# Expert-choice stage with up and down products of two experts alternated on TensorE

## The chip, the cores and the metric

One core of a Trainium2 chip runs the whole kernel. Times are device microseconds of one execution; the kernel before was run three times.

## The reference, cut

The kernel computes two gated transformer layers over 8 x 256 tokens of 256 features: attention, capacity experts, dilated attention, and last the expert-choice stage, the only one that the change touches:

```python
Sm = softmax(xf @ Wr + br)              # 2048 tokens, 8 experts
G_t, idx_t = top_k(Sm.T, 256)           # each expert takes its 256 best tokens
tokens = xf[idx]
Wu = W_up[arange(8) // 2]               # two experts of a group share the up weights
mid = silu(einsum('keh,ehf->kef', tokens, Wu) + bu)      # 256 -> 682
out = einsum('kef,efh->keh', mid, W_down) + b_down       # 682 -> 256
y = zeros_like(xf).at[idx].add(G[..., None] * out)
```

## The kernel before

`experts_choice` (L1895) is the fourth stage. Its first part finds each expert's threshold over the 2048 probabilities by a search in eight levels on VectorE (L2170 to L2192), then ranks the tokens. The weights are loaded on SP meanwhile; SP's first load waits until GpSimd has zeroed `bu_in` and `w2` (L2056, L2057), and VectorE's search starts after constants of GpSimd and after the bias table `buT`, which needs SP's three first loads.

The second part handles eight experts. Products are made exact enough by splitting each float32 operand into a float16 high and low part and multiplying three times (high by high, high by low, low by high). The weights are scaled by 256 before the split.

`pipeline` (L2008) is shared by all engines. It issues `step(e, u, g, slots, rows, products)`: two steps ahead of the loop, a device loop of three iterations with two steps each, two steps behind it. In step e each engine does its share of

- `slots` of expert e + 2: VectorE marks token positions (`at_lo` L2255, `at_hi`, `vhi`), TensorE multiplies them (16 small products into `ps_i`, L2369), VectorE turns the result into indices (`g_idx` L2293, a copy `who` L2294), GpSimd gathers the token rows (L2088);
- `rows` of expert e + 1: ScalarE splits up and down weights (L2132) and VectorE takes their low parts (L2273); TensorE turns the gathered rows in two tiles of 128 tokens (L2362) into the two banks `ps_y`, ScalarE and VectorE split them (L2136, L2278); VectorE copies gate and bias columns (L2283, L2287);
- `products` of expert e: six chunks f of the 682 hidden features. TensorE makes 6 up products of 256 columns per chunk (L2351) into four banks `ps_h`, ScalarE applies silu and copies the high part (L2121, L2126), VectorE takes the low part (L2268). Then TensorE makes 2 x 18 down products (L2384), VectorE adds the bias (L2303), ScalarE scales by the gate (L2142), GpSimd adds the rows into the output with two indirect transfers (L2098).

Every engine runs its instructions in the order of the code. On TensorE that is up(e), with the turning of e + 1 between chunks, slots of e + 2, down(e). The down products wait for the hidden low parts of the same expert, and the second token tile of `ps_y` for the split rows, since `ps_x` and `ps_y` are the same banks. ScalarE and VectorE do weight splits between the chunks f (after f = 0 and 2; f = 1 and 3). There is one `hh`, one `hl`, one `yb`, one `y`, one staging `w1` and one `w2`; SP loads the next pair of weights when both low parts are done.

Of the kernel before, what the change touches and what calls it, by code (L numbers as in the profile page):

```python
# [15 lines left out]
F16 = mybir.dt.float16  # L16
BF16 = mybir.dt.bfloat16
I32 = mybir.dt.int32
# [1876 lines left out]
def experts_choice(nc, S, ins, dram, keep, out):  # L1895
# [7 lines left out]
    LEVELS = [26, 22, 18, 14, 10, 6, 2, 0]  # L1903
    WS = 256.0
    FIRST = 4
    assert GRP == 16 and LAST and E // G == 2 and TAKE <= 512
    ident, ones, tg, prob = keep["ident"], keep["ones"], keep["tg"], keep["prob"]
    with ExitStack() as ctx:
# [52 lines left out]
        g_idx = [sb(f"g_idx{u}", [P, CT], I32) for u in range(2)]  # L1961
        s_idx = [sb(f"s_idx{u}", [P, CT], I32) for u in range(2)]
        who = sb("who", [P, E, CT])
        xg = [sb(f"xg{u}", [P, CT, S.ROW]) for u in range(2)]
        gate = [sb(f"gate{u}", [P, CT]) for u in range(2)]
        b1 = [sb(f"b1{u}", [P, FC]) for u in range(2)]
# [3 lines left out]
        w2 = sb("w2", [P, FC, D])  # L1970
# [4 lines left out]
        h = [sb(f"h{k}", [P, TAKE]) for k in range(2)]  # L1975
        hh = sb("hh", [P, FC, TAKE], F16)
        hl = sb("hl", [P, FC, TAKE], F16)
        yb = sb("yb", [P, CT, D])
        y = sb("y", [P, CT, D])
# [6 lines left out]
        ps_x = [ps_y[k][:, 0:C * P].rearrange("p (c t) -> p c t", c=C) for k in range(2)]  # L1986

        s_cst = sem("cst"); s_byA = sem("byA"); s_abv = sem("abv"); s_si = sem("si"); s_ldb = sem("ldb")
# [8 lines left out]
        s_g = [sem("g0"), sem("g1")]; s_w = sem("w"); s_gate = sem("gate"); s_b1 = sem("b1")  # L1997
        s_px = sem("px"); s_xh = sem("xh"); s_xl = sem("xl"); s_wh = sem("wh"); s_wl = sem("wl")
# [3 lines left out]
        def pipeline(step):  # L2002


            def run(eng):
                step(-2, 0, 0, True, False, False)
                step(-1, 1, 0, True, True, False)
                with eng.Fori(0, E // 2 - 1) as i:  # L2008
                    step(i * 2, 0, i, True, True, True)
                    step(i * 2 + 1, 1, i + 1, True, True, True)  # L2010
                step(E - 2, 0, G - 1, False, True, True)
                step(E - 1, 1, G, False, False, True)
            return run

        def count(eng, what, value):

            if not isinstance(value, int) or value > 0:
                eng.wait_ge(what, value)

# [11 lines left out]
        def _(sp):  # L2031
            bu = ins["L1_ffn_b_up"]
            sp.wait_ge(s_fill, 2)
# [4 lines left out]
            def load(e, g):  # L2038
                sp.dma_start(w1[:], ins["L1_ffn_W_up"][g].rearrange("(c p) f -> p c f", p=P)).then_inc(s_w, 16)
                down = ins["L1_ffn_W_down"][e]  # L2040
                sp.dma_start(w2[:, 0:FULL, :], down[0:FULL * P, :].rearrange("(c p) d -> p c d", p=P))\
                    .then_inc(s_w, 16)
                sp.dma_start(w2[0:LAST, FULL, :], down[FULL * P:F, :]).then_inc(s_w, 16)

            load(0, 0)

            def step(e, u, g, slots, rows, products):
                if rows and not (isinstance(e, int) and e + 2 >= E):
                    sp.wait_ge(s_wl, (e + 2) * 2)
                    load(e + 2, g + 1 if u == 0 else g)  # L2050

            pipeline(step)(sp)

        @block.gpsimd
        def _(pool):
            pool.memset(bu_in[:], 0.0).then_inc(s_fill, 1)  # L2056
            pool.memset(w2[:], 0.0).then_inc(s_fill, 1)  # L2057
# [23 lines left out]
            def step(e, u, g, slots, rows, products):  # L2081
                if slots:
                    pool.wait_ge(s_gi, (e + 3) * 2)
                    count(pool, s_px, (e + 1) * CT)
                    count(pool, s_gate, e + 1)
                    apart(pool, s_pass)
                    for j in range(CT):
                        pool.indirect_dma_start(  # L2088
                            out=xg[u][:, j, :], out_offset=None, in_=dram["rows"],
                            in_offset=bass.IndirectOffsetOnAxis(ap=g_idx[u][:, j:j + 1], axis=0))\  # L2090
                            .then_inc(s_g[u], 16)
                if products:
                    count(pool, s_add, e * CT * 16)
                    pool.wait_ge(s_si, e + 1)
                    for j in range(CT):
                        pool.wait_ge(s_y, e * CT + j + 1)
                        apart(pool, s_pass)
                        pool.indirect_dma_start(  # L2098
                            out=flat_out, out_offset=bass.IndirectOffsetOnAxis(ap=s_idx[u][:, j:j + 1], axis=0),
                            in_=y[:, j, :], in_offset=None, compute_op=ALU.add).then_inc(s_add, 16)  # L2100

            pipeline(step)(pool)
# [3 lines left out]
        def _(act):  # L2106
            act.wait_ge(s_pt, 2)
            for k in (1, 3):
                act.wait_ge(s_pt, k + 1)
                act.activation(byexp[:, k * 512:(k + 1) * 512], ps_t[:, k, :], ACT.Copy).then_inc(s_byA, 1)  # L2110

            def step(e, u, g, slots, rows, products):
                v = 1 - u
                if products:
                    act.wait_ge(s_b1, e + 1)
                for f in range(FC):
# [321 lines left out]
```

## Time and profile before

| | |
|---|---|
| median of 3 runs | 938.09 us (936.34 to 939.6) |
| the profiled execution, own time | 939.1 us |
| its span, first to last instruction | 937.4 us |
| mean granted TensorE clock | 0.833 |
| busy: TensorE, VectorE, ScalarE, GpSimd | 654.0, 528.3, 427.8, 338.0 us |
| first up product of the expert-choice stage | 798.1 us |

The page divides the span into 40 slices; the product part of the last stage is the last six (23.4 us each). A digit is the busy share in tenths:

```profile
PE   3999983145999999999324877788877301757755
DVE  0467753625656666564025578877755387555651
ACT  1344430034567775576112546566555110564652
PEclk9999995557999999999755788998888555787877
```

### The profile page before, as it was taken

What the parts mean: (1) busy time and instruction counts of PE and PEld (TensorE: products, weight loads), DVE (VectorE), ACT (ScalarE), POOL (GpSimd) and SP (SyncE); (2) the same over time, 40 slices, a digit from 0 to 9 for tenths busy, and PEclk for the clock granted to TensorE, in tenths of its full rate; (3) what the DMA queues carried; (4) which work ended last, traced back from release to release, by engine and by line L of the source; (5) the groups of instructions that cost most, each with busy time, mean ns of one, the idle gap of its engine ahead of it and who ended that gap; (6) DMA issues with size and microseconds to landing.
All of it is one profiled execution on the core that took longest, in us unless ns stands there. A gap on an engine that the chain in (4) does not pass through costs nothing. (4 is left out here: it accounts for less than half of the span.)

```text
span 937.4 us, 15352 instructions
## 1 busy us (share of the span) xinstructions
PE 654.0 (70%) x4856; PEld 486.4 (52%) x4856; DVE 528.3 (56%) x1701; ACT 427.8 (46%) x847; POOL 338.0 (36%) x473
## 2 busy tenths in 40 slices
PE   3999983145999999999324877788877301757755
PEld 3888872123877778777212444455445200545543
DVE  0467753625656666564025578877755387555651
ACT  1344430034567775576112546566555110564652
POOL 1244431053653466452212444544433201323422
PEclk9999995557999999999755788998888555787877
DMA  5132321334453455441311212332100110435332
GB/s 174 45 124 84 121 91 45 125 94 134 103 136 82 121 130 113 126 78 23 50 40 41 70 42 80 92 93 62 45 25 34 71 59 14 146 89 153 89 86 23
DMA packets 74955, 78.66 MB, mean 84 GB/s; under 512 B 8101, under 2 KB 66513, under 8 KB 74641
## 3 DMA queue, kind: packets, MB, share of 16 engines
q1 hardware_dynamic: 62305, 62.11, 21.0%
q0 software_dynamic: 10928, 15.57, 9.7%
q8 instruction: 28, 0.46, 0.2%
q10 hardware_dynamic: 1664, 0.27, 0.2%
q14 instruction: 30, 0.25, 0.1%
HBM read 54.99 MB, written 22.94 MB: 83 GB/s over the span
## 5 line engine op out<-in xcount | busy, mean ns | idle before, releaser
L1650 DVE CUSTOM_DVE_ANT_0 c_sn<-c_ps_s,k_mask 128x128 f32<-128x128 f32 (+1 forms) x256 | 75.8, 352 | 57.7 <-PE c_ps_s L1788 57.6
L1174 PE MATMUL b_ps_y<-b_w2h,b_hh 128*128 128x256 f16 x320 | 87.3, 273 | 4.5 <-DVE b_xl L1050 4.2
L924 POOL DMA_INDIRECT res<-b_y,b_s_idx x40 | 72.7, 1816 | 42.4 <-ACT b_y L966 30.8
L1174 PE MATMUL b_ps_y<-b_w2l,b_hh 128*128 128x256 f16 x320 | 87.2, 273 | 0.0
L1174 PE MATMUL b_ps_y<-b_w2h,b_hl 128*128 128x256 f16 x320 | 87.2, 273 | 0.0
L910 POOL DMA_INDIRECT b_xg<-rows,b_g_idx x40 | 43.8, 1094 | 119.7 <-DVE b_g_idx L1068 110.0
L1482 POOL TENSOR_SCALAR_AFFINE_SELECT c_pr<-c_pr 128x512 f32<-128x512 f32 x64 | 42.9, 671 | 111.0 <-ACT c_pr L1541 110.0
L1041 DVE TENSOR_TENSOR b_hl<-b_h,b_hh 128x640 f16<-128x640 f32 x64 | 52.8, 825 | 36.9 <-ACT b_hh L946 36.7
L1816 PE MATMUL c_ps_v<-c_pr,k_vx 128*64 128x256 f32 (+1 forms) x512 | 64.0, 377 | 5.5 <-POOL c_pr L1482 4.9
L1139 PE MATMUL b_ps_h<-b_xh,b_w1h 128*128 128x320 f16 x256 | 57.1, 305 | 12.7 <-ACT b_h L941 9.3
L941 ACT ACTIVATE b_h<-b_ps_h,b_b 128x640 f32<-128x640 f32 x64 | 50.1, 784 | 18.8 <-DVE b_hl L1041 11.6
L1541 ACT ACTIVATE c_pr<-c_ps_t 128x768 f32<-128x768 f32 x64 | 51.7, 807 | 13.2 <-PE c_ps_t L1802 13.2
L1139 PE MATMUL b_ps_h<-b_xl,b_w1h 128*128 128x320 f16 x256 | 56.9, 304 | 0.0
L1139 PE MATMUL b_ps_h<-b_xh,b_w1l 128*128 128x320 f16 x256 | 56.9, 304 | 0.0
L2384 PE MATMUL d_ps_y<-d_w2h,d_hh 128*128 128x256 f16 x96 | 34.2, 357 | 31.2 <-DVE d_xl L2278 30.9
L1788 PE MATMUL c_ps_s<-k_ks,c_qs 48*128 48x128 f16 (+1 forms) x256 | 25.3, 282 | 43.4 <-DVE c_mx L1650 27.9
L2088 POOL DMA_INDIRECT d_xg<-rows,d_g_idx x16 | 18.6, 1165 | 98.1 <-DVE d_who L2294 95.6
L966 ACT ACTIVATE b_y<-b_yb,b_gate 128x256 f32<-128x256 f32 x40 | 20.3, 508 | 72.6 <-DVE b_yb L1087 72.6
L1816 PEld LDWEIGHTS c_ps_v<-c_pr,k_vx 128*64 128x64 f32 x512 | 34.6, 152 | 30.7 <-issue 12.6
L946 ACT ACTIVATE b_hh<-b_h 128x640 f16<-128x640 f32 x64 | 47.2, 737 | 2.3
L2098 POOL DMA_INDIRECT out_dram<-d_y,d_s_idx x16 | 29.5, 1845 | 37.3 <-ACT d_y L2142 30.2
L1788 PEld LDWEIGHTS c_ps_s<-k_ks,c_qs 48*128 48x128 f16 x256 | 10.1, 104 | 51.5 <-DVE c_mx L1650 21.0
(382 smaller groups left out, 1812.2 us busy)
## 6 DMA issues: line engine op xcount, KB each, us to landing
b_w<-in_L_ffn_W_dram SPq DMA_DIRECT2D x16, 1024.0 KB, 5.6
d_w<-in_L_ffn_W_up_dram SPq DMA_DIRECT2D x8, 682.0 KB
d_w<-in_L_ffn_W_down_dram SPq DMA_DIRECT2D x8, 640.0 KB
k_ks<-kT SPq DMA_DIRECT2D x48, 64.0 KB, 2.5
c_qs<-q SPq DMA_DIRECT2D x48, 64.0 KB, 2.3
rows<-a_rows SPq DMA_DIRECT2D x8, 264.0 KB, 2.5
rows<-c_rows SPq DMA_DIRECT2D x8, 264.0 KB, 2.2
a_x_in<-in_x_dram SPq DMA_DIRECT2D x8, 256.0 KB, 3.0
```

What stands on the lines that cost most here:

```text
L910: pool.indirect_dma_start(out=xg[u][:, j, :], out_offset=None, in_=dram["rows"], in_offset=bass.IndirectOffsetOnAxis(ap=g_idx[u][:, j:j + ...
L924: pool.indirect_dma_start(out=dram["res"], out_offset=bass.IndirectOffsetOnAxis(ap=s_idx[u][:, j:j + 1], axis=0), in_=y[:, j, :], in_offse ...
L941: act.activation(h[f % 2][:], ps_h[f % 2][:, :, 0:HALF], ACT.Gelu, bias=b1[u][:, f:f + 1], scale=1.0 / WS).then_inc(s_h, 1)
L946: act.activation(hh[:, f, :], h[f % 2][:].rearrange("p a b -> p (a b)"), ACT.Copy)\
L1041: dve.tensor_tensor(hl[:, f, :], h[f % 2][:].rearrange("p a b -> p (a b)"), hh[:, f, :], ALU.subtract).then_inc(s_hl, 1)
L1139: last = pe.matmul(ps_h[f % 2][:, t, 0:HALF], a, b[:, c, t * HALF:(t + 1) * HALF], start=(c == 0 and k == 0), stop=(c == C - 1 and k == 2))
L1174: last = pe.matmul(ps_y[(j + CT) % 2][:, 0:D], a, b[:, f, :], start=(f == 0 and k == 0), stop=(f == FC - 1 and k == 2))
L1482: pool.affine_select(out=late, in_=late, compare_op=ALU.is_ge, fill=0.0, base=0, pattern=[[0, 2], [0, 2], [1, P]], channel_multiplier=-1). ...
L1541: act.activation(pr[i % 2][:], ps_t[:, :, 0:QK], ACT.Exp).then_inc(s_pr, 1)
L1650: dve.tensor_tensor_reduce(sn[r][:, a:b], ps_s[:, r, a:b], mask[:, a:b], -1.0, 3.0e38, ALU.add, ALU.min, mx[g % 2][:, q, r, j:j + 1]).then ...
L1788: last = pe.matmul(ps_s[:, r, lo:hi], q[a:a + 3 * HD, j, rows_], key[a:a + 3 * HD, j, 0:keys], start=True, stop=True)
L1816: last = pe.matmul(ps_v[VW * r:VW * (r + 1), 0:b - a], vx[n % 2][:, part, 2 * j + r, :], pr[i % 2][:, r, a:b], start=(part == 0), stop=(pa ...
```

## The change

The assertions now ask for 2 token tiles, an even number of chunks, and 512 columns for `C * TAKE`. `pipeline` and the device loop go: every engine's order is written for e from -1 to 7 with Python loops, and all instructions are unrolled. TensorE's order is up(e+1), turn(e+2), slots(e+3), down(e). Chunks are handled in pairs: two silus, one copy and one subtraction of 2 x 256 columns. The rows of an expert are turned in one go into the bank `ps_r` and split whole. The up split is made once per group of two experts. The gate is read from the gathered rows and the bias from `buT` by ScalarE itself; the scatter uses the same index tile as the gather. There are now two each of `w2`, `hh`, `hl`, `y`, four of `xg`, five of `g_idx`, and one `w1` as before. ScalarE runs one silu on a single column at the start of the stage. The diff, cut:

```diff
@@ tiles and banks
+        g_idx = [sb(f"g_idx{u}", [P, CT], I32) for u in range(5)]
+        xg = [sb(f"xg{u}", [P, CT, S.ROW]) for u in range(4)]
         w1 = sb("w1", [P, C, F])
-        w2 = sb("w2", [P, FC, D])
+        w2 = [sb(f"w2{u}", [P, FC, D]) for u in range(2)]
-        h = [sb(f"h{k}", [P, TAKE]) for k in range(2)]
+        h = [sb(f"h{k}", [P, 2, TAKE]) for k in range(2)]
+        hh = [sb(f"hh{u}", [P, FC, TAKE], F16) for u in range(2)]
+        hl = [sb(f"hl{u}", [P, FC, TAKE], F16) for u in range(2)]
+        yb = [sb(f"yb{j}", [P, D]) for j in range(CT)]
+        y = [sb(f"y{u}", [P, CT, D]) for u in range(2)]
-        ps_x = [ps_y[k][:, 0:C * P].rearrange("p (c t) -> p c t", c=C) for k in range(2)]
+        ps_x = ps_r[:, 0:C * TAKE].rearrange("p (c t) -> p c t", c=C)
@@ SP
-            sp.wait_ge(s_fill, 2)
+            sp.wait_ge(s_fill, 3)
...
+            load_up(0)
+            load_down(0)
+            load_down(1)
+            for e in range(E):
+                if e % 2 == 0 and group(e) + 1 < G:
+                    sp.wait_ge(s_wl1, group(e) + 1)
+                    load_up(group(e) + 1)
+                if e + 2 < E:
+                    sp.wait_ge(s_wl2, e + 1)
+                    load_down(e + 2)
@@ GpSimd
-            pool.memset(w2[:], 0.0).then_inc(s_fill, 1)
+            for u in range(2):
+                pool.memset(w2[u][:], 0.0).then_inc(s_fill, 1)
...
+            def gather(e):
+                pool.wait_ge(s_gi, e + 1)
+                count(pool, s_y, (e - 3) * CT)
...
+            def scatter(e):
+                count(pool, s_add, e * CT * 16)
+                for j in range(CT):
+                    pool.wait_ge(s_y, e * CT + j + 1)
...
+            for e in range(-3, E):
+                if e + 3 < E:
+                    gather(e + 3)
+                if e >= 0:
+                    scatter(e)
@@ ScalarE
+            act.wait_ge(s_warm, 1)
+            act.activation(warm[:], warm[:], ACT.Silu)
+
+            def up_high(g):
+                act.wait_ge(s_w1, (g + 1) * 16)
+                count(act, s_ph, (g - 1) * 2 * FC)
+                act.activation(w1h[g % 2][:], w1[:], ACT.Copy, scale=WS).then_inc(s_wh1, 1)
+
+            def down_high(e):
+                act.wait_ge(s_w2[e % 2], (e // 2 + 1) * 32)
+                count(act, s_py, (e - 1) * CT)
+                act.activation(w2h[e % 2][:], w2[e % 2][:], ACT.Copy, scale=WS).then_inc(s_wh2, 1)
+
+            def hidden(e, p):
...
+                for q in range(2):
...
+                    act.wait_ge(s_ph, e * FC + f + 1)
+                    if q == 0:
+                        count(act, s_hl, n - 1)
+                    act.activation(h[n % 2][0:r, q, :], ps_h[f % 4][0:r, 0:TAKE], ACT.Silu,
+                                   bias=buT[0:r, f * G + group(e):f * G + group(e) + 1], scale=1.0 / WS)\
+                        .then_inc(s_h, 1)
+                act.wait_ge(s_h, e * FC + 2 * p + 2)
+                count(act, s_py, (e - 1) * CT)
+                act.activation(hh[e % 2][:, 2 * p:2 * p + 2, :], h[n % 2][:], ACT.Copy).then_inc(s_hh, 1)
...
+            up_high(0)
+            act.wait_ge(s_buT, 1)
+            rows_high(0)
+            for e in range(-1, E):
+                if e + 1 < E:
+                    for p in range(PAIRS):
+                        hidden(e + 1, p)
+                    if e + 2 < E:
+                        rows_high(e + 2)
+                    down_high(e + 1)
+                    if e % 2 == 1 and group(e + 3) < G:
+                        up_high(group(e + 3))
+                if e >= 0:
+                    scaled(e)
@@ VectorE
+            def found(e):
+                dve.wait_ge(s_pidx, e + 1)
+                count(dve, s_add, (e - 4) * CT * 16)
+                dve.tensor_scalar(g_idx[e % 5][:], ps_i[:, 0:CT], -1.0, 0.0, ALU.add, ALU.max).then_inc(s_gi, 1)
...
+            marked(0)
+            found(0)
+            marked(1)
+            up_low(0)
+            found(1)
+            marked(2)
+            rows_low(0)
+            for e in range(-1, E):
+                if e + 4 < E:
+                    marked(e + 4)
+                if e + 1 < E:
+                    hidden_low(e + 1, 0)
+                if e >= 0:
+                    down_low(e)
+                if e + 1 < E:
+                    hidden_low(e + 1, 1)
+                if e >= 0 and e % 2 == 0 and group(e + 2) < G:
+                    up_low(group(e + 2))
+                if e + 1 < E:
+                    hidden_low(e + 1, 2)
+                if e + 2 < E:
+                    rows_low(e + 2)
+                if e + 3 < E:
+                    found(e + 3)
+                if e >= 0:
+                    biased(e)
@@ TensorE
+            def hidden(e):
+                g = group(e)
+                pe.wait_ge(s_xl, e + 1)
+                pe.wait_ge(s_wl1, g + 1)
+                for f in range(FC):
+                    r = rows_of(f)
+                    count(pe, s_h, e * FC + f - 3)
...
+            def down(e):
+                pe.wait_ge(s_wl2, e + 1)
+                for j in range(CT):
+                    count(pe, s_yb, (e - 1) * CT + j + 1)
+                    for f in range(FC):
+                        r = rows_of(f)
+                        if j == 0 and f % 2 == 0:
+                            pe.wait_ge(s_hl, e * PAIRS + f // 2 + 1)
...
+            found(0)
+            found(1)
+            turned(0)
+            for e in range(-1, E):
+                if e + 1 < E:
+                    hidden(e + 1)
+                if e + 2 < E:
+                    turned(e + 2)
+                if e + 3 < E:
+                    found(e + 3)
+                if e >= 0:
+                    down(e)
```

Helpers not shown: `rows_high` and `rows_low` split `ps_x` with one instruction each; `marked` issues `at_lo`, `at_hi` and `vhi`; `up_low` and `down_low` are the weights' low parts; `hidden_low(e, p)` is the low part of a pair of chunks; `biased` and `scaled` handle the two token tiles of a result, `biased` waiting for the end of each tile's down products; `turned` makes four transposes after its gather has landed.

## Rows read from the trace of the kernel before

**Rows 1.** Two loop steps: length; busy PE, PEld, DVE, ACT, POOL; clock; DMA share; GB/s.

```profile
817.20:851.90 34.70, 24.23 (x186) 17.12 (x184) 19.52 (x41) 19.02 (x38) 11.65 (x8) 0.80 0.44 112
```

**Rows 2.** Chain of waits, last stage: start us, length, what.

```profile
789.51 0.88 issue
...
820.96 1.47 ACT d_w2h L2132
...
823.61 0.80 DVE d_w2l L2273
...
826.09 7.25 PE d_ps_y L2384 x36
```

**Rows 3.** Windows of 1 us; columns as in rows 1, the clock third from last.

```profile
806.00:807.00 1.00, 0.49 (x17) 0.40 (x15) 0.55 (x2) 0.97 (x3) 0.00 (x0) 1.00 0.00 0
808.00:809.00 1.00, 0.00 (x0) 0.00 (x0) 1.00 (x3) 0.57 (x2) 0.00 (x0) 0.60 0.00 0
831.00:832.00 1.00, 1.00 (x6) 0.74 (x5) 0.14 (x1) 0.51 (x1) 0.00 (x0) 0.50 0.52 137
832.00:833.00 1.00, 1.00 (x10) 0.68 (x8) 0.00 (x0) 0.00 (x0) 0.39 (x1) 0.95 0.04 13
```

**Rows 4.** Timeline of TensorE: start us, length, idle before.

```profile
798.14 0.39 PE L2351 MATMUL d_ps_t<-d_xh,d_w1h 128*128 128x256 f16 x1 [0.53 <-DVE d_xl L2278]
...
801.32 0.31 PE L2351 MATMUL d_ps_t<-d_xh,d_w1h 128*128 128x256 f16 x1
...
802.88 0.27 PE L2351 MATMUL d_ps_t<-d_xh,d_w1l 128*128 128x256 f16 x1
804.54 0.44 PE L2362 MATMUL d_ps_y<-ident,d_xg 128*128 128x128 f32 x2 [1.39 <-DMA d_xg<-rows,d_g_idx]
...
805.95 0.54 PE L2369 MATMUL d_ps_i<-d_vhi,d_at_lo 128*128 128x2 f16 x16
```

**Rows 5.** Groups by line and shape: count, busy, mean ns, idle before.

```profile
L2121 ACT ACTIVATE d_h<-d_ps_t,d_b 128x256 f32<-128x256 f32 x40 | 18.3, 457 | 0.0
L2255 DVE TENSOR_TENSOR d_at_lo<-d_lane,d_lo 128x2048 f16<-128x2048 f16 x8 | 18.3, 2286 | 0.5 <-issue 0.4
L2268 DVE TENSOR_TENSOR d_hl<-d_h,d_hh 128x256 f16<-128x256 f32 x40 | 16.9, 423 | 17.8 <-ACT d_hh L2126 17.8
L2126 ACT ACTIVATE d_hh<-d_h 128x256 f16<-128x256 f32 x40 | 16.7, 416 | 1.5
L2273 DVE SCALAR_TENSOR_TENSOR d_w2l<-d_w,d_w2h 128x1536 f16<-128x1536 f32 x8 | 14.0, 1752 | 0.0
...
L2283 DVE COPY d_gate<-d_xg 128x2 f32 x6 | 0.9, 151 | 0.0
...
L1041 DVE TENSOR_TENSOR b_hl<-b_h,b_hh 128x640 f16<-128x640 f32 x64 | 52.8, 825 | 36.9 <-ACT b_hh L946 36.7
```

**Rows 6.** ScalarE's table loads (window from 735 us); SP's issue of one pair of weights.

```profile
L2121 ACT ACT_TABLE_LOAD x3 | 3.8, 1283 | 0.8 <-DVE d_b L2287 0.8
...
825.39 0.38 SPq L2039 DMA_DIRECT2D d_w<-in_L_ffn_W_up_dram  x1
```

**Rows 7.** GpSimd's timeline, and issue to landing of its gathers, then its scatters.

```profile
799.17 2.21 POOL L2088 DMA_INDIRECT d_xg<-rows,d_g_idx  x1 [4.87 <-DVE d_who L2294]
801.68 0.95 POOL L2088 DMA_INDIRECT d_xg<-rows,d_g_idx  x1 [0.30 <-issue]
...
815.46 1.64 POOL L2098 DMA_INDIRECT out_dram<-d_y,d_s_idx  x1 [2.19 <-ACT d_y L2142]
...
DMA to landing us min/median/max: 2.7/3.9/4.2
...
DMA to landing us min/median/max: 3.7/3.8/4.9
```

**Rows 8.** Timeline of the tail.

```profile
927.87 0.42 DVE L2303 SCALAR_TENSOR_TENSOR d_yb<-d_ps_y,d_bd 128x256 f32<-128x256 f32 x1 [1.75 <-PE d_ps_y L2384]
```

**Rows 9.** Timeline of the stage's start.

```profile
743.34 1.37 POOL L2057 MEMSET d_w<- 128x1536 f32 x1
```

More of the change, by code:

```diff
@@ L2036, in _, with load_up, load_down @@
             sp.dma_start(bd[:], ins["L1_ffn_b_down"].partition_broadcast(P)).then_inc(s_ldb, 16)
[L2038 to L2039 removed]
+            def load_up(g):
+                sp.dma_start(w1[:], ins["L1_ffn_W_up"][g].rearrange("(c p) f -> p c f", p=P)).then_inc(s_w1, 16)
+            def load_down(e):
                 down = ins["L1_ffn_W_down"][e]
[L2041 to L2052, printed above, removed]
+                sp.dma_start(w2[e % 2][:, 0:FULL, :], down[0:FULL * P, :].rearrange("(c p) d -> p c d", p=P))\
+                    .then_inc(s_w2[e % 2], 16)
+                sp.dma_start(w2[e % 2][0:LAST, FULL, :], down[FULL * P:F, :]).then_inc(s_w2[e % 2], 16)
+            load_up(0)
[8 more added lines that the diff above has]
+                    load_down(e + 2)
         @block.gpsimd
@@ new lines, in rows_low, with biased @@
+            def rows_low(e):
+                dve.wait_ge(s_xh, e + 1)
+                dve.tensor_tensor(xl[e % 2][:], ps_x, xh[e % 2][:], ALU.subtract).then_inc(s_xl, 1)
+            def biased(e):
+                count(dve, s_y, e * CT)
+                for j in range(CT):
+                    dve.wait_ge(s_py, e * CT + j + 1)
+                    dve.scalar_tensor_tensor(out=yb[j][:], in0=ps_y[j][:, 0:D], scalar=1.0 / WS,
+                                             in1=bd[:, e, :], op0=ALU.mult, op1=ALU.add).then_inc(s_yb, 1)
@@ L2388, in _ @@
-            pipeline(step)(pe)
+                    count(pe, s_h, e * FC + f - 3)
+                    if e and f < 2:
+                        pe.wait_ge(s_h, e * FC)
+                    for c in range(C):
+                        hi, lo = w1h[g % 2][:, c, f * P:f * P + r], w1l[g % 2][:, c, f * P:f * P + r]
+                        for k, (a, b) in enumerate(((hi, xh[e % 2]), (hi, xl[e % 2]), (lo, xh[e % 2]))):
+                            last = pe.matmul(ps_h[f % 4][0:r, 0:TAKE], a, b[:, c, :],
+                                             start=(c == 0 and k == 0), stop=(c == C - 1 and k == 2))
@@ new lines, in hidden, with turned, found @@
+                    last.then_inc(s_ph, 1)
+            def turned(e):
+                pe.wait_ge(s_g[e % 2], (e // 2 + 1) * CT * 16)
+                count(pe, s_xl, e)
+                for j in range(CT):
+                    for c in range(C):
+                        last = pe.transpose(ps_x[:, c, j * P:(j + 1) * P], xg[e % 4][:, j, c * P:(c + 1) * P], ident[:])
+                last.then_inc(s_px, 1)
+            def found(e):
+                pe.wait_ge(s_vhi, e + 1)
+                pe.wait_ge(s_atlo, e + 1)
+                count(pe, s_gi, e)
+                for i in range(NT):
+                    last = pe.matmul(ps_i[:, 0:CT], at_lo[e % 2][:, i, :], vhi[e % 2][:, i, :],
+                                     start=(i == 0), stop=(i == NT - 1))
+                last.then_inc(s_pidx, 1)
```

241 lines of the change are left out of this document (59 added, 182 removed).

## The prediction, made before the changed kernel was run

> **What bounds the kernel now.** The change lies in the last stage alone, so I read that stage and not the page's shares. One look at the window of two loop steps gives 34.7 us for two experts, with TensorE busy 24.2, VectorE 19.5, ScalarE 19.0, GpSimd 11.7, at a mean granted clock of 0.80 [rows 1]. No engine is full: it is a chain. The chain of waits shows which: up products, then ScalarE's split of the next expert's down weights (1.47), VectorE's low part and the split rows, then 36 down products in 7.25 us [rows 2]. TensorE's own order is strict: up(e), down(e). Between them it stands still while ScalarE and VectorE finish hidden rows, weight splits and split rows that they do in one queue.
>
> The second loss is the clock. At 806 to 807 us the granted clock is still full while TensorE falls idle; within 808 to 809 it drops to half, and after the restart it stays half until 832 in the next step [rows 3]. Those two levels are 2.4 and 1.2 GHz. On TensorE's timeline 15 products start between 798.14 and 801.32 (0.213 us each, half clock), then 14 up to 802.88 (0.11, full clock) [rows 4]. So 36 products are 7.7 us or 3.95 us. The 7.25 us of down products [rows 2] are 28 at half and 8 at full clock, 6.85, and 0.4 for the changes to and from 42 rows: 4.3 at full clock.
>
> **The new round, part by part.** Round e: TensorE does up(e+1), turns the rows of e+2, finds the slots of e+3, does down(e). The down products' inputs are a round old, so their wait for VectorE's hidden rows goes. What is late next must be read off the other engines.
>
> *TensorE*, full clock: 3.95 + 0.8 (four transposes, 0.44 for two) + 0.55 (slots) + 4.3 = 9.6 us [rows 4].
>
> *VectorE*. Instructions issued back to back overlap by 0.09. Marks: 2.29 + two small ones, 2.65 together. A 512-wide hidden low part is not in the trace; between the 256-wide 0.42 and stage b's 640-wide 0.83 I take 0.69, nearest the wider row. Three of them 1.8 net; down low part 1.66 net; up low part (1364 of 1536 columns) 1.5, now every second round; split rows 0.6, like a hidden part; slots 0.1; biased results 2 x 0.35 [rows 5, 8]. That is 7.5 (9.0 with the up part). Removed are the gate, bias, slot and two index copies of 0.15 (0.07 net each), some 0.4 us.
>
> *ScalarE*. Six activations of 0.46 (0.37 net, 0.49 before a wait) and three 512-wide copies of 0.63 (bounds 0.42 and twice that; the fixed part is paid once): 4.2 us. Rows 0.6, down split 1.4 net, up split 1.3 every second round (1364 of 1536 columns), two results 1.0 (256 wide, like an activation of 0.46): 7.2 (8.5) [rows 2, 5]. Two of the three table loads of 1.28 us, one per loop iteration, leave the path; the third is taken early beside the threshold search [rows 6].
>
> *GpSimd*. Two gathers of 0.95 and two scatters of 1.6 with gaps, about 6.2 us a round [rows 7]: not the bound.
>
> Three cross waits set the round. (a) down(e) needs down_low(e), which stands in VectorE's queue behind the biased result of e-1, the marks and one hidden part: 0.2 + 0.35 + 2.65 + 0.6 + 1.75 = 5.6 us after TensorE's last down product, against 5.3 of TensorE's own work. Round: 5.6 + 4.3 = 9.9. (b) The gather: slots found(e+3) come last in VectorE's round (7.4 us in, 8.9 with an up part); 0.9 us of issue, 0.95 + 0.3 for the first of two gathers, and 2.7 to 4.2 us from the second's issue to its landing are 4.9 to 6.4 us [rows 2, 7]; beside the marks 1.3 more. I take 5.1 where VectorE and the weights' transfers rest, else 6.6. TensorE wants the rows 13.8 us in: no stall in an ordinary round, 0.2 to 1.7 with an up part. The surcharge is read from one gather beside the marks, 2.21 us, and the next one without them, 0.95 [rows 7]. The Trainium skill (SBUF — State Buffer, Who interferes with whom) reports that tensor_copy stalled such DMAs and tensor_tensor did not; the trace disagrees, since the marks are a tensor_tensor. By that rule the sum would be about 2 us lower. (c) The third wait is new and speaks against the change. There is one w1 buffer, and SP issues the up weights of group 2 and 3 only after the down weights of experts 3 and 5, thus after down_low(1) and down_low(3). From issue to the end of traffic such a pair took 6.1 us (825.39 to 831.5) [rows 3, 6]. ScalarE asks for them in the same round, between the down split and the scaled results: it stands from 7.4 to about 11.7 us, counted from the start of rounds 1 and 3. The activations of the next expert are queued behind, so TensorE stops after four PSUM banks, about 1.9 us, and VectorE's low part comes another 2 us late.
>
> **The sum**, on the axis of the profiled execution.
> - Stage start: a second memset of 1.37 us sits before SP's loads and the constants [rows 9]; the search waits for both. First up products 798.1 [rows 4] + 1.4 + 0.4 (rows split whole) = 799.9. Below nothing only if neither is waited for; at most 2 x 1.4.
> - up(0) starts at half clock. The clock came back 3.3 us after the restart at 798.1 [rows 4] and 6 us after that at 826.1 [rows 2, 3]; I take 5.1 of half clock: 6.4 us, 806.3. Transposes, split rows: up(1) at 808.9, ends 812.8. ScalarE's up split of group 1 is in its way but inside the four banks.
> - The slots of 2 are found at 809.0 and VectorE goes straight on to marks: the gather lands 815.6. Turn and slots: down(0) starts 817.0, after an idle time like those that cost the clock: 4.3 + 2.55. Round 0 ends 823.85.
> - Round 1, ordinary: 9.9, 833.75. Its up weights land at 829.45 + 6.1 = 835.55, ScalarE is free at 837.8.
> - Round 2: fifth up group at 838.3 instead of 836.4, up(3) ends 839.4, hidden part 839.85, down_low 841.6, down 4.3: 845.95, 12.2 us. Round 3: gather 5 lands 851.0 against 849.85: 10.75. Round 4, wait (c) again, without marks: 11.25. Rounds 5 and 6, without marks: 9.3 and 9.05. Together 62.45: 886.3.
> - down(7): nothing sets its low part ahead of the biased result of 6: 0.55 + 1.75 = 2.3, + 4.3: 892.9.
> - Tail: 9.5 us from the last biased result to the end (927.9 to 937.4) [rows 8]. The scatters of 7 wait for those of 6 to land: the second of 6 issues near 888.9 and lands up to 4.9 us later (median 3.8) [rows 7], where 7's first would issue at 892.0: + 1.7. 904.1.
> - Clock lost again in about half of rounds 2, 3 and 4, at 2.55 each, part of it used by engines that were late: + 3. End of span **907**.
>
> That is 30 us below the span of 937.4. The profiled execution is 939.1, the median of the runs 938.1: the profiled execution becomes 908.7 and, 1.0 lower, the forecast is 908 beside the median; the rivals' times below are their spans + 0.7 in the same way.
>
> **Rivals.**
> 1. *Everything hides.* The clock stays full after its first rise and rounds close at 9.9. For: each engine's sum is under 9.9. Against: wait (c) is written into the queues. 817.0 + 4.3 + 6 x 9.7 + 6.6 + 9.5 = 895.6, time 896.
> 2. *A clock dip in every round.* TensorE idles 1.4 to 3.3 us between up and down products in each. For: the idle 1.39 us before 804.54 and the one from 806.5 on were enough for the drop at 808 [rows 3, 4]. Against: most gaps are filled by transposes and slots. Eight rounds at 10.4 + 2.55 = 13: 817.0 + 6.9 + 6 x 13 + 9.1 + 11.2 = 922.2, time 923. The Trainium skill (TensorE: Matmul & The Clock Gate, A second HAM failure mode: psum-queue depth-cycling) tells of a kernel whose short idles between matmul groups made the clock swing. The trace agrees that it can swing in this stage; how often it would in the new order no row shows.
> 3. *Slower: the clock never returns.* Place: TensorE in the product rounds. At half clock a round is 7.7 + 1.1 + 0.6 + 7.9 = 17.3 us: 799.9 + 8 x 17.3 + 2.3 + 9.5 = 950, time 951. It decides once more than some 85% of the products run at half clock. Against: down(e) and up(e+2) are 8 us without a wait, and rows 3 and 4 show the clock back in 6 at most.
> 4. *The change does not do what it says*: TensorE's order is written out, so it alternates; what could fail is only the overlap, which is a waiting round as before (17 us), no gain: 938.
>
> **Numbers.** Forecast case (900 to 914) 0.52; rival 1 0.20; rival 2 0.22; rival 3 0.03; rival 4 0.03. From no change a measurement here tells 0.3%, 2.8 us. Range: down to 894 for rival 1 with cheaper 512-wide instructions (three at 0.6 instead of 0.69), up to 923 for most of rival 2. Faster 0.95, same 0.02, slower 0.03.
>
> **What would show it.** Timeline of TensorE: up, four transposes, 16 slot products, down, in 9 to 12 us a round. The waits: ScalarE's w1h waiting for the up weights' DMA twice, about 4 us each; down products waiting for w2l; one or two transposes waiting for a gather; the last down group waiting 2.3 us. Granted clock of the stage near 0.85 to 0.9; near 1.0 means rival 1, at 0.75 with dips in each round rival 2. The forecast is wrong if the search stage starts more than 2 us later, if GpSimd becomes the engine that all wait for, or if rounds 2 and 4 are no longer than the others.

## The result, and the profile after

The changed kernel takes 908.71 us (907.44 to 912.67, four runs) against 938.85 us of the kernel before in four runs: a ratio of 0.968, 95% interval 0.964 to 0.972. The forecast was 908, made up of a span 30.4 us shorter; the median is 30.1 us lower. One execution of run tail below took 3370 us, which no trace explains; its ratio leaves it out.

The profiled execution took 912.67 us, its span is 911.0. The table below cuts the last stage of a span in two: from GpSimd's first memset of the stage to the first up product (the *head*), and from there to the end of the span (the *products*, tail included). What lies ahead of the stage is the same code in all kernels and ended between 741.3 and 749.8 us in the fourteen profiles, with no order that I can explain; so parts of a stage are compared, not spans.

| | head | products | stage |
|---|---|---|---|
| before | 54.9 | 139.3 | 194.2 |
| after | 59.0 | 102.3 | 161.2 |

The stage is 33.0 us shorter. The first fence is the window of the product rounds of the kernel before, the second that of the kernel after (length; busy PE, PEld, DVE, ACT, POOL; clock; DMA share; GB/s).

```profile
798.00:928.00 130.00, 94.72 (x700) 66.78 (x700) 69.30 (x149) 71.27 (x142) 41.57 (x29) 0.80 0.40 101
```

```profile
808.70:901.50 92.80, 78.74 (x700) 59.96 (x700) 56.69 (x79) 59.34 (x105) 43.39 (x27) 0.96 0.41 99
```

The 700 instructions on TensorE are the same in number. Its busy time fell by 16 us, because the granted clock rose from 0.80 to 0.96 of 2.4 GHz, and its idle time fell from 35 to 14 us. TensorE's timeline of rounds 1 to 3, after (the figure in brackets is the idle time before, and its releaser):

```profile
829.32 0.28 PE L2373 MATMUL d_ps_t<-d_xh,d_w1h 128*128 128x256 f16 x1
...
833.47 0.66 PE L2382 MATMUL d_ps_r<-ident,d_xg 128*128 128x128 f32 x4
...
835.18 0.28 PE L2404 MATMUL d_ps_y<-d_w2h,d_hh 128*128 128x256 f16 x1 [0.68 <-DVE d_w2l L2284]
...
839.52 0.28 PE L2373 MATMUL d_ps_t<-d_xh,d_w1h 128*128 128x256 f16 x1
...
847.42 0.28 PE L2404 MATMUL d_ps_y<-d_w2h,d_hh 128*128 128x256 f16 x1 [0.86 <-DVE d_w2l L2284]
...
851.77 0.28 PE L2373 MATMUL d_ps_t<-d_xh,d_w1h 128*128 128x256 f16 x1
...
857.24 0.66 PE L2382 MATMUL d_ps_r<-ident,d_xg 128*128 128x128 f32 x4 [1.26 <-DMA d_xg<-rows,d_g_idx]
```

The order is up, turn, slots, down as forecast; the counterpart before is the single stretch of 7.25 us of [rows 2]. In rounds 1 and 2 the down products wait 0.7 and 0.9 us for the low part of their weights, in round 3 the turn of rows waits 1.3 us for its gather. Rounds 1 to 6 last 10.2, 12.25, 10.7, 11.9, 9.45 and 9.45 us. The waits of the stage (us in total, times, longest):

```profile
PE d_ps_r L2382 <- DMA d_xg<-rows,d_g_idx: 8.8, 3, 5.3
ACT d_w1h L2113 <- DMA d_w<-in_L_ffn_W_up_dram: 7.8, 2, 4.2
...
PE d_ps_y L2404 <- DVE d_w2l L2284: 5.8, 6, 2.2
...
POOL out_dram L2089 <- DMA out_dram<-d_y,d_g_idx: 2.9, 1, 2.9
```

ScalarE's wait for the up weights' transfer, twice, 7.8 us together, is wait (c) of the prediction. On ScalarE's timeline it stands between the down split and the scaled results:

```profile
836.36 1.47 ACT L2118 ACTIVATE d_w2h<-d_w 128x1536 f16<-128x1536 f32 x1
841.46 1.34 ACT L2113 ACTIVATE d_w1h<-d_w 128x1364 f16<-128x1364 f32 x1 [3.63 <-DMA d_w<-in_L_ffn_W_up_dram]
842.70 0.89 ACT L2143 ACTIVATE d_y<-d_yb,d_xg 128x256 f32<-128x256 f32 x2
```

The clock, in windows of 1 us (columns as above). The stage's first up products, from 808.7, ran at half clock until 813. With TensorE idle from 821.84 to 824.09 the clock stayed full; it fell once, at 895.5, when the last down products waited 2.2 us for down_low(7):

```profile
823.00:824.00 1.00, 0.00 (x0) 0.00 (x0) 1.00 (x3) 0.50 (x1) 0.00 (x0) 1.00 0.42 118
895.00:896.00 1.00, 0.44 (x3) 0.32 (x4) 0.50 (x1) 0.00 (x0) 0.82 (x1) 0.54 0.69 55
```

### The profile page after: what moved, and what is told of

It reads as the page before. It is cut to its first block and busy times, and to the rows that moved or that the text cites. A ratio compares the mean times of both kernels' runs of the same rounds, so it can differ in the third digit from the quotient of the medians.

```text
span 911.0 us, 14874 instructions
## 1 busy us (share of the span) xinstructions
PE 643.9 (71%) x4856; PEld 481.8 (53%) x4856; DVE 517.4 (57%) x1634; ACT 415.2 (46%) x810; POOL 338.9 (37%) x474
## 5 line engine op out<-in xcount | busy, mean ns | idle before, releaser
L924 POOL DMA_INDIRECT res<-b_y,b_s_idx x40 | 67.6, 1691 | 44.0 <-ACT b_y L966 34.2
L1816 PE MATMUL c_ps_v<-c_pr,k_vx 128*64 128x256 f32 (+1 forms) x512 | 66.4, 388 | 5.3 <-POOL c_pr L1482 4.9
L2079 POOL DMA_INDIRECT d_xg<-rows,d_g_idx x16 | 21.4, 1335 | 73.7 <-DVE d_g_idx L2275 70.7
L2089 POOL DMA_INDIRECT out_dram<-d_y,d_g_idx x16 | 31.6, 1976 | 22.5 <-ACT d_y L2143 16.2
L297 POOL TENSOR_TENSOR a_rstd<-a_var,a_half 128x2 f32<-128x2 f32 x16 | 11.4, 716 | 70.3 <-DVE a_var L432 70.3
L1139 PEld LDWEIGHTS b_ps_h<-b_xh,b_w1h 128*128 128x128 f16 x256 | 23.5, 99 | 26.5 <-ACT b_h L941 15.5
```

Source lines behind the costliest of these rows:

```text
L924: pool.indirect_dma_start(out=dram["res"], out_offset=bass.IndirectOffsetOnAxis(ap=s_idx[u][:, j:j + 1], axis=0), in_=y[:, j, :], in_offse ...
L1139: last = pe.matmul(ps_h[f % 2][:, t, 0:HALF], a, b[:, c, t * HALF:(t + 1) * HALF], start=(c == 0 and k == 0), stop=(c == C - 1 and k == 2))
L1816: last = pe.matmul(ps_v[VW * r:VW * (r + 1), 0:b - a], vx[n % 2][:, part, 2 * j + r, :], pr[i % 2][:, r, a:b], start=(part == 0), stop=(pa ...
L2089: pool.indirect_dma_start(out=flat_out, out_offset=bass.IndirectOffsetOnAxis(ap=g_idx[e % 5][:, j:j + 1], axis=0), in_=y[e % 2][:, j, :], ...
```

## The experiments

Twelve runs followed, one of them the changed kernel once more. All figures in us; the time is the median of a run's executions, the ratio is to the kernel before on the same chip. The runs stood on different chips, so times are compared by their ratios.

| run | time | ratio (95%) | head | products |
|---|---|---|---|---|
| again (the change) | 906.2 | 0.964 (0.960 to 0.969) | 58.8 | 103.0 |
| serial | 939.5 | 0.999 (0.996 to 1.003) | 58.8 | 135.0 |
| early | 904.0 | 0.962 (0.958 to 0.967) | 58.8 | 97.3 |
| tail | 906.0 | 0.965 (0.958 to 0.971) | 58.6 | 100.9 |
| serial2 | 900.4 | 0.959 (0.955 to 0.962) | 59.1 | 94.7 |
| unroll | 935.8 | 0.999 (0.997 to 1.001) | 55.2 | 135.8 |
| filler | 925.7 | 0.987 (0.984 to 0.991) | 55.4 | 126.4 |
| best | 903.9 | 0.965 (0.963 to 0.967) | 54.2 | 105.5 |
| alt2 | 906.0 | 0.966 (0.963 to 0.969) | 58.8 | 101.9 |
| moved | 909.9 | 0.971 (0.968 to 0.975) | 59.1 | 106.0 |
| spliteach | 947.4 | 1.010 (1.006 to 1.014) | 59.0 | 144.6 |
| best2 | 895.2 | 0.956 (0.953 to 0.958) | 54.3 | 94.7 |

### again: the same kernel

> The changed kernel itself once more, so that the edits below have it on the same chip. From the first up product to the end of the span its profile had 102.3 us (before: 139.3), from the start of the last stage 161.2 us (before: 194.2). Expected again within 2 us of both; the time 905 to 912, since the three earlier stages, which the change doesn't touch, differed by 6.6 us between the two profiles.

Head 58.8, products 103.0, as expected. Its earlier stages ended at 747.9. One thing differs from the first profile: behind the wait of 2.3 us for the gather of expert 2 the clock fell to half, and down(0) took 6.0 us instead of 4.4.

```profile
821.38 0.66 PE L2382 MATMUL d_ps_r<-ident,d_xg 128*128 128x128 f32 x4 [2.34 <-DMA d_xg<-rows,d_g_idx]
```

```profile
824.00:825.00 1.00, 1.00 (x6) 0.46 (x5) 0.00 (x0) 0.04 (x1) 0.51 (x1) 0.50 0.15 49
```

### serial: the order undone

```diff
-                if e >= 0:
-                    down(e)
+                if e + 1 < E:
+                    down(e + 1)
```

with `down_low(e + 1)`, `biased(e + 1)` and `scaled(e + 1)` at the end of the same round on VectorE and ScalarE.

> The changed kernel with one thing undone: TensorE does down(e) right behind up(e), as before; VectorE and ScalarE do down_low, biased and scaled of the same expert in the same round. Splits shared by a group, pairs of chunks, buffers and unrolling stay. Theory A (the order gives the gain, by filling the gap and through it by the clock): a round is 3.95 of up products, then hidden rows, down split and its low part up to 9.2 us, then 4.3 to 7 of down products: 14 to 16 us, first up product to end 122 to 138 us, time 928 to 944, the granted clock dips in each round. Rival B (fewer and wider instructions and no device loop give most of it): at most 112 us, time 910 to 918.

The whole gain in time is gone: the ratio is 0.999. Shared splits, 512-wide instructions, more buffers and unrolling together leave the products about 4 us shorter than before the change, and the head about 4 us longer. TensorE's timeline of the run, and the window of its rounds:

```profile
824.58 0.54 PE L2389 MATMUL d_ps_i<-d_vhi,d_at_lo 128*128 128x2 f16 x16
829.19 0.40 PE L2403 MATMUL d_ps_y<-d_w2h,d_hh 128*128 128x256 f16 x1 [4.07 <-DVE d_w2l L2284]
```

```profile
802.60:928.00 125.40, 92.54 (x700) 66.69 (x700) 57.67 (x78) 59.44 (x105) 40.45 (x27) 0.82 0.30 73
```

Rival B fell. But the line behind the down products names w2l and not hl: the wait that came back, 3.9 to 4.4 us in each of the eight rounds, is that for the low part of the down weights, which this edit had also moved.

### serial2: the strict order, the down split one expert ahead

```diff
 # against serial; ScalarE
-                    down_high(e + 1)
+                    down_high(e + 2)      # inside "if e + 2 < E"
 # VectorE
-                    down_low(e + 1)
-                    biased(e + 1)
+                if e + 2 < E:
+                    down_low(e + 2)
+                if e + 1 < E:
+                    biased(e + 1)
```

with `down_high(0)` and `down_low(0)` ahead of the loop.

> The kernel of run serial (TensorE strictly up(e), down(e)) with the split of the down weights made one expert ahead: down_high(e+2) and down_low(e+2) in the round of up(e+1). TensorE stood 3.9 to 4.4 us for w2l before each group of down products in run serial. Theory A (the alternated order is what gives the gain): the down products now wait for the hidden low parts of their own expert, a dip of the clock stays, rounds of 12 to 14 us, first up product to end 110 to 122 us. Theory C (the gain is that the down split leaves the wait; the order only did that): the last pair of hidden low parts is ready 6.1 us into the round, when TensorE, after up products, transposes and slots (5.3 us), is at the third chunk of the down products and needs the fifth; rounds of 9.9 to 10.8 us, full clock, first up product to end 98 to 106 us, as with the change.

94.7 us of products: 40 us less than serial, and 8 less than the change, with TensorE in the order of the kernel before. That is below the range of theory C as well (98 to 106). Theory A fell, theory C stands. TensorE's timeline, and its window:

```profile
816.78 0.28 PE L2375 MATMUL d_ps_t<-d_xh,d_w1h 128*128 128x256 f16 x1
...
822.15 0.66 PE L2384 MATMUL d_ps_r<-ident,d_xg 128*128 128x128 f32 x4 [1.16 <-DMA d_xg<-rows,d_g_idx]
...
827.39 0.28 PE L2375 MATMUL d_ps_t<-d_xh,d_w1h 128*128 128x256 f16 x1
```

```profile
805.30:887.00 81.70, 76.59 (x700) 58.94 (x700) 55.59 (x77) 58.36 (x104) 46.99 (x26) 0.97 0.46 108
```

Up to down(6) no down product waits for a hidden low part; down(7) waits 0.55 us. The other idle time between the rounds is for gathers, 0.2 to 1.7 us, 4.4 in all. The split ahead also asks for the weights a round earlier, so wait (c) does not show, and the strict order has down(0) to do between up(0) and up(1): it starts its first down products 7.1 us after the first up products, the changed kernel 16.3.

### alt2: the alternated order with the low part out of the way

```diff
-                if e >= 0:
-                    down_low(e)
...
+                if e + 1 < E:
+                    down_low(e + 1)
                 if e >= 0:
                     biased(e)
```

> The changed kernel, alternated order kept, with down_low(e+1) made in round e ahead of the biased results, where run serial2 has its own (there it is e+2 and the order up(e), down(e)). Down products then never wait for it, and the weights' loads are asked for a round earlier, so wait (c) goes too. Theory C (with the splits out of the way either order does): first up product to end 93 to 98 us (serial2: 94.7, the change: 102.3 and 103.0). Theory A' (alternation gives something more of its own, since no hidden part is ever waited for): 90 us or less.

101.9, above the ranges of both theories. The waits for the up weights are gone, and so are those for w2l but for one of 0.5 us, but the gather takes their place, most at the start, and the clock fell behind it (half speed into the following down products, which took 5.9 us, and once more in round 3, 6.0 us):

```profile
818.87 0.66 PE L2382 MATMUL d_ps_r<-ident,d_xg 128*128 128x128 f32 x4 [3.53 <-DMA d_xg<-rows,d_g_idx]
...
825.66 0.28 PE L2373 MATMUL d_ps_t<-d_xh,d_w1h 128*128 128x256 f16 x1
```

So alternation has no gain of its own here. It costs the start of the pipeline: up(1) waits 1.6 us for the split rows of expert 1 and the next turn 3.5 us for its gather, with no other products to do. These 5.1 us and the two spells of half clock, 3.1 us, are the 7.2 us against serial2, within 1 us.

### moved: one edit to the kernel before

```diff
 # ScalarE: behind the loop over f
-                    if rows and f in (0, 2):
-                        ...
+                if rows:
+                    act.wait_ge(s_w, (e + 2) * 48)
+                    count(act, s_py, e * CT)
+                    for stage, high in ((w1, w1h[v]), (w2, w2h[v])):
+                        act.activation(high[:], stage[:], ACT.Copy, scale=WS).then_inc(s_wh, 1)
```

and VectorE's two low parts likewise, behind the slots' indices.

> The kernel before with one edit: ScalarE's two weight splits stand behind all hidden chunks and split rows instead of behind chunks 0 and 2, VectorE's two low parts behind the slots' indices. Loop, buffers, widths, two splits for each expert and the strict order stay. Theory C: the 4.6 to 5 us between up and down products shrink to 1.5 to 2.5 us, ScalarE's 2.8 and VectorE's 3.3 us go beside the down products, and the clock stays or dips less: rounds of 11 to 13 us against 17, first up product to end 100 to 115 us, time 898 to 913. Rival E (the split rows in the banks of ps_y keep the down products waiting, and the low parts then hold up the next up products): 125 us or more.

106.0 us of products: 33.3 of the 37.0 us that the change takes from this part, with loop, buffers, widths, unshared splits and order all as before. The head grew from 54.9 to 59.1 us, since the first up products now wait 4.7 us for weights' low parts, so the stage is 29.1 us shorter against the change's 33.0; the ratio is 0.971 against 0.968 and 0.964. What the down products waited for, before and in this run (us in total, times, longest):

```profile
PE d_ps_y L2384 <- DVE d_xl L2278: 30.9, 7, 5.0
```

```profile
PE d_ps_y L2383 <- DVE d_xl L2272: 4.7, 6, 1.4
```

TensorE's timeline, and its window:

```profile
825.63 0.27 PE L2350 MATMUL d_ps_t<-d_xh,d_w1h 128*128 128x256 f16 x1 [0.81 <-DVE d_w2l L2292]
...
833.32 0.28 PE L2383 MATMUL d_ps_y<-d_w2h,d_hh 128*128 128x256 f16 x1 [1.36 <-DVE d_xl L2272]
```

```profile
801.20:897.50 96.30, 80.17 (x700) 59.44 (x700) 69.82 (x144) 69.91 (x141) 48.48 (x27) 0.97 0.54 140
```

The 2.8 to 5.0 us before the down products are 1.4 us at most, and the clock is 0.97. ScalarE and VectorE are as busy as before: their work did not shrink, it only left the place where TensorE waited.

### filler: the clock by itself

```diff
+                    for _ in range(36):
+                        pe.matmul(ps_r[:, 0:TAKE], w1h[u][:, 0, 0:P], xh[u][:, 0, :], start=True, stop=True)
```

> The kernel before with 36 more products of 256 columns into an unused bank behind the slots and before the down products of every expert, from operands that are ready. They fill 3.9 us of TensorE's wait at full clock, so the clock should stay and nothing else change: it prices the clock alone. Theory A: down products 4.4 us instead of 6.6 to 7.3 in seven experts, 15 to 20 us less from first up product to end (139.3), time 919 to 924, so half of the change's gain. Rival D (the clock is the whole gain): 30 us less or more. Rival: the added products are in the way, 0 to 5 us less.

12.9 us less, under theory A, but that is a net figure. Counted from the first up product of one expert to that of the next, the first seven rounds are 16.4 us shorter together: their down products take 4.4 us. That is within theory A. In the last round nothing was idle before down(7), so there the added products are in the way, and up(7) and down(7) take 12.5 us instead of 9.1 (last two rows below). In round 0 they make the down products start 1.0 us later. Waits that the clock does not touch are left: the down products' for VectorE's split rows (0.71 us in the second row), and two of the up products' for ScalarE (1.07 us each).

```profile
835.14 4.09 PE L2374 MATMUL d_ps_r<-d_xh,d_w1h 128*128 128x256 f16 x36
839.94 0.28 PE L2386 MATMUL d_ps_y<-d_w2h,d_hh 128*128 128x256 f16 x1 [0.71 <-DVE d_xl L2278]
...
906.42 4.10 PE L2374 MATMUL d_ps_r<-d_xh,d_w1h 128*128 128x256 f16 x36
...
910.36 0.27 PE L2386 MATMUL d_ps_y<-d_w2h,d_hh 128*128 128x256 f16 x1
```

```profile
798.00:918.00 120.00, 108.35 (x988) 86.47 (x988) 69.48 (x148) 71.73 (x143) 43.76 (x30) 0.98 0.44 110
```

The clock alone is thus worth some 16 to 17 of the 37 us, a little under half, and not the whole; the rest is idle time.

### unroll: the loop alone

```diff
-                with eng.Fori(0, E // 2 - 1) as i:
+                for i in range(E // 2 - 1):
```

> The kernel before, its device loop replaced by a Python loop, nothing else. Theory A: two of three table loads of 1.28 us and the loop's branches go, 2.6 to 4 us less of 139.3 from first up product to end, time 934 to 937. Rival B (the loop costs much more than it shows, in branches on five engines and instruction loading): 8 us less or more.

3.5 us less in the products, within theory A, with one table load of 1.28 us in the place of three; in the time, 0.999 with 1 inside the interval.

### early: wait (c)

```diff
-                if e % 2 == 0 and group(e) + 1 < G:
-                    sp.wait_ge(s_wl1, group(e) + 1)
-                    load_up(group(e) + 1)
+                if e in (0, 1, 3):
+                    sp.wait_ge(s_wl1, (e + 1) // 2 + 1)
+                    load_up((e + 1) // 2 + 1)
```

> SP issues the up weights of groups 2 and 3 one round earlier, ahead of the down weights of experts 3 and 5. Theory A with wait (c) of the prediction: ScalarE no longer waits 4 us for them in rounds 1 and 3, rounds 2 and 4 shrink from 12.3 and 11.9 us to 10.2 to 10.7: 3 to 3.5 us less from first up product to end, about 99 us. Rival: the gather or the down low part is late by nearly as much, and under 1 us is won.

97.3, 5.0 and 5.7 us less than the two profiles of the change. Round 2 is 9.7 us instead of 12.25 (838.37 to 848.10), round 4 is 9.45 instead of 11.9:

```profile
838.37 0.28 PE L2373 MATMUL d_ps_t<-d_xh,d_w1h 128*128 128x256 f16 x1
...
843.75 0.28 PE L2404 MATMUL d_ps_y<-d_w2h,d_hh 128*128 128x256 f16 x1 [0.20 <-DVE d_w2l L2284]
...
848.10 0.28 PE L2373 MATMUL d_ps_t<-d_xh,d_w1h 128*128 128x256 f16 x1
```

Wait (c) is real, and cost more than the 3 to 3.5 expected.

### tail: down_low(7) earlier

```diff
-                if e >= 0:
+                if 0 <= e < E - 1:
                     down_low(e)
...
+                if e + 2 == E:
+                    down_low(E - 1)
                 if e >= 0:
                     biased(e)
```

> down_low(7) stands ahead of the biased results of expert 6 on VectorE. By the prediction's term the last down products start 2.2 us earlier and stay at full clock (1.9 us more): about 4 us less. Rival, from the trace after: the scatters are a chain of their own, each pair waits until the pair before has landed; the first of expert 6 began at 893.25 after waiting for that of 5, so the last pair can begin no earlier than about 900.2 against 901.5: 1 to 1.5 us less, whatever TensorE wins. The rival is the likelier.

100.9: 1.4 and 2.1 less. The last down products end about 4 us earlier against the first up product, and GpSimd then waits for the landing of the pair before:

```profile
887.71 1.55 POOL L2089 DMA_INDIRECT out_dram<-d_y,d_g_idx  x1 [3.84 <-ACT d_y L2143]
...
894.18 1.55 POOL L2089 DMA_INDIRECT out_dram<-d_y,d_g_idx  x1 [3.06 <-DMA out_dram<-d_y,d_g_idx]
```

From this pair to the next 6.5 us go by. In serial2 and best2, where GpSimd waits for a landing three times in a row, it is 6.4 to 7.6 us; the longer ones have a first scatter of 2.3 to 2.6 us instead of 1.55.

### spliteach: the up split for each expert (the edit missed its aim)

SP, ScalarE and VectorE handle the up weights once per expert, `w1h[e % 2]` instead of `w1h[g % 2]`.

> The changed kernel with the up weights loaded and split for each expert, as before the change (ScalarE 1.33 and VectorE 1.57 us more in every second round); the load is asked for a round earlier, so wait (c) is gone as in run early (97.3 us from first up product to end). Theory C: sharing saves work beside TensorE's, so 97 to 101 us. Rival B (less work is the gain): 105 us or more.

1% slower than the kernel before. My edit put the load of the next up weights behind a down load that waits for down_low(e), so it did not remove wait (c) but made one in every round, and `up_low` stood ahead of `rows_low` on VectorE. The waits:

```profile
PE d_ps_t L2373 <- DVE d_xl L2295: 37.2, 8, 6.0
...
ACT d_w1h L2113 <- DMA d_w<-in_L_ffn_W_up_dram: 22.7, 6, 5.0
```

It says nothing on the price of sharing, which stays open. It shows what wait (c) does when it comes in six rounds: ScalarE waits 22.7 us for it, TensorE 37.2 us for split rows queued behind it, and more than the change's gain is lost.

### best and best2: the start, and what then bounds

best is the change with the edits of early and tail, another order on VectorE, and two edits at the stage's start:

```diff
-            sp.wait_ge(s_fill, 3)
+            sp.wait_ge(s_fill, 1)
...
             load_up(0)
+            sp.wait_ge(s_fill, 3)
             load_down(0)
             load_down(1)
+            sp.wait_ge(s_g[0], CT * 16)
```

with the memsets of w2 behind the constants. best2 is serial2 with the same start and `up_low` behind the slots' indices.

> The changed kernel with four edits: up weights issued a round earlier (run early); down_low(7) ahead of the last biased results but one (run tail); in VectorE's round down_low(e), the first hidden part, then the marks, instead of marks, hidden part, down_low(e); and at the stage's start the two memsets of w2 behind the constants, SP's first loads waiting for bu_in alone, and the second up weights issued after the first gather has landed. Expected against the change, from stage start to end 161.5: 5 to 5.5 from early, 1 to 2 from tail, 1.5 to 3 from the order (down products start 5.3 instead of 5.6 us in), 2 to 4 at the start: 148 to 152, time 894 to 899. Rival: the chain of scatters (a pair, its landing, the next pair) takes over as the bound; then 153 to 155.

> Run serial2 with up_low of the next group moved behind the slots' indices, so that the gather of every second round starts 1.5 us earlier (TensorE waited 0.2 to 1.7 us for a gather in six rounds, 4.4 us in all behind the first), and with the start edits of run best, which brought the first up product from 58.8 to 54.2 us after the stage's start. Expected: stage 146 to 149 us (serial2: 153.8), time 892 to 897. Rival: the scatters, each pair waiting for the landing of the one before, already end serial2 13.5 us behind the last down product instead of 9.5; then only the start's 4.6 us less what the chain of scatters keeps, 150 to 152.

The start works in both: heads of 54.2 and 54.3 instead of 59.0. Still best missed its forecast and its rival: its stage takes 159.7 us, against 148 to 152 and 153 to 155. Its products went up to 105.5: down products wait for w2l only once, 0.5 us, but three gathers are waited for, 9.5 us in all, with dips of the clock behind two of them. The slots are not found later (7.6 us into round 1, 7.9 in the change). The gathers land later: the half awaited below was issued at 834.65, took GpSimd 2.4 us, and landed while 682 KB of down weights, issued at 836.25, were on the way. Which of the two delayed it was not tried.

```profile
841.20 0.66 PE L2386 MATMUL d_ps_r<-ident,d_xg 128*128 128x128 f32 x4 [2.96 <-DMA d_xg<-rows,d_g_idx]
```

best2 has the lowest median and the lowest ratio of all that ran, 0.956 against 0.968 and 0.964 of the change, and its stage takes 148.9 us, as forecast. In the ratio its interval overlaps that of serial2; in the stage it is 4.9 us shorter. All of that is the start; its products are 94.7 as well. Its gathers are waited for as long as before, and its scatters bound the end: the three such waits of the stage.

```profile
POOL out_dram L2091 <- DMA out_dram<-d_y,d_g_idx: 9.2, 3, 3.1
...
PE d_ps_r L2386 <- DMA d_xg<-rows,d_g_idx: 4.3, 5, 1.3
```

## Why the prediction was right, point by point

- **The net.** 30.4 us forecast, 30.1 measured. That is better than its terms, which erred on both sides, and in part luck: the stage, where the whole forecast lies, got 33.0 us shorter (194.2 to 161.2), and on the chip of run again the medians lay 33.9 us apart.
- **The head** was mis-sized: + 1.8 forecast, + 4.0 measured. The search starts 1.7 us later (1.4 forecast), the split rows cost 0.6 (0.4 forecast). The rest is a term that I left out: the first gather landed 5.0 us after its second half was issued, against 3.1 before, with SP issuing the second up weights 0.5 us behind it. In best and best2, which hold these weights back, it landed after 3.2. The start edits together took 4.6 to 4.8 us off: by the trace of best, 3.0 at the start of the search and 1.8 at the gather.
- **Up to the first down products**: 17.1 forecast, 16.3 measured, the gather of expert 2 as late as forecast.
- **The clock** was the wrong step. I charged 2.55 us in round 0 and 3 more for dips in rounds 2 to 4. None came in this profile: the idle time in the rounds was 0.3 to 2.3 us, and the clock stood. In run again, the same kernel, it fell in round 0, at a cost of 1.6 us. In both it fell where I had charged nothing, before down(7). The granted clock of the product rounds is 0.96; the sign that I gave was 0.85 to 0.9 for the stage.
- **Rounds 1 to 6**: 62.45 forecast, 64.0 measured, one by one 9.9, 12.2, 10.75, 11.25, 9.3, 9.05 against 10.2, 12.25, 10.7, 11.9, 9.45, 9.45. Waits (a), (b) and (c) are where the queues said they would be; run early confirms (c).
- **down(7) and tail**: 6.6 + 11.2 forecast; 8.1 + 9.6 measured. The wait for down_low(7) was 2.2 us as forecast (2.3), and the half clock cost another 1.5. The tail is shorter than forecast, since the scatters of 7 do not wait for a landing here: they come after the late down(7). Run tail, with down(7) earlier, brings that wait out, 3.06 us.
- **The reason** for the gain was only half right. I wrote that the down products' inputs are a round old, "so their wait for VectorE's hidden rows goes". But the trace before has 30.9 us of down products waiting for the split rows of the next expert, and 0.3 us for hidden rows; serial2, whose inputs are not a round old, waits 0.55 us for hidden rows in all. The split rows were late because two weight splits on ScalarE and two low parts on VectorE stood ahead of them in the queues, among the hidden parts. Run moved settles it: it moves these splits alone, keeps the order, and 30.9 us become 4.7. The change works because it takes the splits out of that queue, and the alternation is a way to do so, not the best one.
- Rival 3 did not come. Of rival 1 the clock came, nearly full, and the rounds did not: two of them took 12.25 and 11.9 us. Rival 2's mechanism showed at the end of the product rounds, and in round 0 of run again.
- The surcharge of 1.3 us for gathers beside the marks was about right. The four gathers of the changed kernel that GpSimd began while VectorE was marking took 1.95 to 2.41 us, those that it began with VectorE idle 0.94 to 1.02. The Trainium skill (SBUF — State Buffer, Who interferes with whom) tells of a probe in which a tensor_tensor, which the marks are, did not stall such transfers; these rows speak against it. Of reads the same section says that a tensor_tensor with two inputs in SBUF contends with those of GpSimd.

## What to carry to other kernels

When an engine waits at the join of two others, list what stands in their queues between the last input it had and the one it waits for; work that nobody needs yet belongs behind that join. Moving two splits within their queues was worth nine tenths of this rewrite, 29.1 of the 33.0 us of the stage. Before a pipeline is made deeper, look at what the extra stage costs at both ends (up(1) with nothing beside it, a chain of scatters that waits for landings) and at which load is now asked for last.

## What the runs showed of the hardware that I had not expected

A second memset on GpSimd lengthened a copy on VectorE that doesn't depend on it. The copy took 3.35 us beside one memset of 1.37 us and 4.62 us beside two of 2.68 us together, 1.27 us more for 1.31 us more. In best, where these memsets stand later, the same copy took 1.99 us. The first two rows are from the changed kernel, the third from best:

```profile
749.83 4.62 DVE L2164 COPY d_spread<-prob 128x2048 f32<-128x2048 f32 x1
749.90 2.68 POOL L2050 MEMSET d_w<- 128x1536 f32 x2
```

```profile
745.52 1.99 DVE L2166 COPY d_spread<-prob 128x2048 f32<-128x2048 f32 x1
```

The Trainium skill (SBUF — State Buffer, Who interferes with whom) says that the two engines share a port pair which one instruction holds whole; the trace agrees.

The length of an idle stretch on TensorE did not decide the clock by itself. In the changed kernel one of 2.25 us left it full at 822 us, and one of 2.2 us ended in half clock at 895.5. The same stretch of code went both ways: ahead of the gather of expert 2, 2.34 us of idle time was followed by half clock in again, and 2.33 us in early was not.
